# Second layer of a graph network: scores and context as half-array tiles of TensorE, one per graph

## What is computed

```python
q = heads(x @ Wq + bq); k = heads(x @ Wk + bk); v = heads(x @ Wv + bv)   # 6 heads of 128
scores = einsum('bhqd,bhkd->bhqk', q, k) / sqrt(128)     # per graph: 64 x 64
probs  = softmax(scores + where(adj, 0.0, -9e15), axis=-1)
ctx    = einsum('bhqk,bhkd->bhqd', probs, v)
x      = layernorm(x + ctx.reshape(...) @ Wf + bf)
```

## Time and profile before

| | |
|---|---|
| median of three runs | 3291.2 us |
| lowest, highest | 3290.34, 3293.18 us |
| profiled execution, span from first to last instruction | 3285.7 us |
| PE busy | 3071.5 us, 93% |
| weight loads (PEld) busy | 2970.4 us, 90% |
| DVE busy | 1692.9 us, 52% |
| ACT busy | 1407.6 us, 43% |
| mean granted TensorE clock | 0.985 |

### The profile page before, as it was taken

The page is one execution under the profiler, slowest core; times in us unless marked ns, Lnnn a source line. Parts: engine busy times, 40 slices in busy tenths (PEclk is TensorE's granted clock), DMA queues, the critical chain, the costliest instruction groups (busy, mean ns, idle before and its releaser), DMA issues.

```text
span 3285.7 us, 55951 instructions
## 1 busy us (share of the span) xinstructions
PE 3071.5 (93%) x20800; PEld 2970.4 (90%) x20800; DVE 1692.9 (52%) x3820; ACT 1407.6 (43%) x4261; POOL 843.8 (26%) x457
## 2 busy tenths in 40 slices
PE   6999999999999994699999999999999999999998
PEld 6888888888888883699999999999999999999998
DVE  4777777777777775342343433433423334334334
ACT  4677666766676665322322323223223223232232
POOL 2555655565556554000000000000000000000000
PEclk9999999999999996799999999999999999999999
DMA  2111111111111112201010010010010100100100
GB/s 97 40 39 39 44 43 39 39 44 43 39 39 44 44 39 71 94 24 36 21 40 20 21 40 20 21 40 20 25 35 20 40 21 20 40 21 21 39 20 20
DMA packets 60261, 120.07 MB, mean 37 GB/s; under 512 B 22208, under 2 KB 22208, under 8 KB 60096
## 3 DMA queue, kind: packets, MB, share of 16 engines
q1 hardware_dynamic: 60096, 117.50, 10.5%
HBM read 67.15 MB, written 50.33 MB: 36 GB/s over the span
## 4 chain that ended last, share of the span: by engine, by line
PE 54%; DVE 2%; ACT 2%; DMA 1%; issue 1%; SPq 0%; DVEq 0%; ACTq 0%
PE L_ps_k L117 13%; PE L_ps_q L117 13%; PE L_ps_a L117 12%; PE L_ps_a L954 10%; PE L_ps_s L917 3%; PE L_ps_c L937 2%; ACT L_probs L723 1%; DVE L_cT_lo L812 1%; ACT L_cT_hi L709 1%; DVE L_logits L788 1%; PE L_ps_q L871 0%; PE L_ps_s L871 0%; PE L_ps_k L871 0%; PE L_ps_pt L924 0%; DVE L_neg_max L794 0%
## 5 line engine op out<-in xcount | busy, mean ns | idle before, releaser
L681 POOL TENSOR_TENSOR L_x_tok<-L_x_tok,L_bf_all 128x768 f32<-128x768 f32 x64 | 116.5, 1840 | 1793.3 <-PE L_ps_s L871 1793.3
L788 DVE SCALAR_TENSOR_TENSOR L_logits<-L_ps_s,L_mask 64x256 f32<-64x256 f32 x192 | 81.0, 422 | 804.3 <-PE L_ps_s L917 801.3
L117 PE MATMUL L_ps_k<-L_xT_hi,L_w_hi 128*128 128x256 f32 x1152 | 331.1, 287 | 0.0
L117 PE MATMUL L_ps_q<-L_xT_hi,L_w_hi 128*128 128x256 f32 x1152 | 328.5, 285 | 0.0
L117 PE MATMUL L_ps_k<-L_xT_hi,L_w_lo 128*128 128x256 f32 x1152 | 326.0, 283 | 0.0
L117 PE MATMUL L_ps_q<-L_xT_hi,L_w_lo 128*128 128x256 f32 x1152 | 326.0, 283 | 0.0
L117 PE MATMUL L_ps_k<-L_xT_lo,L_w_hi 128*128 128x256 f32 x1152 | 325.9, 283 | 0.0
L117 PE MATMUL L_ps_q<-L_xT_lo,L_w_hi 128*128 128x256 f32 x1152 | 325.9, 283 | 0.0
L745 ACT COPY L_v_tok<-L_ps_a 128x384 f32<-128x384 f32 x128 | 61.3, 479 | 556.8 <-PE L_ps_a L117 556.8
L323 ACT ACTIVATE L_probs<-L_logits,L_neg_max 128x64 f32<-128x64 f32 x768 | 256.2, 336 | 94.5 <-DVE L_neg_max L446 94.5
L117 PE MATMUL L_ps_h<-L_w_hi,L_xT_hi 128*128 128x384 f32 x768 | 271.2, 353 | 21.2 <-DVE L_w_lo L106 21.2
(11 more groups left out here) (119 smaller groups left out, 8156.3 us busy)
## 6 DMA issues: line engine op xcount, KB each, us to landing
L_x_tok<-x SPq DMA_DIRECT2D x64, 384.0 KB, 2.8
x_scratch<-L_x_out SPq DMA_DIRECT2D x64, 384.0 KB, 2.3
L_x_tok<-x_scratch SPq DMA_DIRECT2D x32, 768.0 KB, 4.2
out<-L_x_tok SPq DMA_DIRECT2D x32, 768.0 KB, 3.4
L_stage<-W SPq DMA_DIRECT2D x6, 384.0 KB, 5.2
L_stage<-H_t SPq DMA_DIRECT2D x6, 384.0 KB, 4.0
L_x_tok<-Wq SPq DMA_DIRECT2D x6, 384.0 KB, 3.6
L_x_tok<-Wk SPq DMA_DIRECT2D x6, 384.0 KB, 3.7
```

The lines of the kernel that those rows point to most:

```text
L117: ins = pe.matmul(out, left[a][c], right[b][c], start=(n == 0), stop=(n == len(terms) - 1))
L681: pool.tensor_tensor(x_tok[:, s, t], x_tok[:, s, t], bf_all[:, :], ALU.add).then_inc(biased, 1)
L788: dve.scalar_tensor_tensor(out=logits[r].rearrange("p (h t) m -> p h t m", t=GT), in0=ps_s[r, :].rearrange("p (h t m) -> p h t m", h=2, t= ...
```

## The change

Scores are computed per graph: for each head and tile two matmuls, one for each graph, with 64 columns of the stationary operand and 64 moving ones. The first graph's output lies in partitions 0 to 63, the second's in 64 to 127, so they are two tiles of 128 rows by 64 columns of the array. All scores of a pair now fill 128 partitions by 256 columns; `ps_s` and `ps_pt` are the halves of one bank, `ps_sp`. Context is likewise two matmuls, with a contraction over the graph's 64 nodes (64 rows by 128 columns of the array), all 128 head columns as the stationary side and 64 moving ones; the two graphs write to two banks of `ps_c`. `probsT` is 64 wide, without zeros, and its memset goes. Logits are one instruction. `context_hi` reads both banks in one instruction per head, `context_lo` has one instruction per head and tile. Scores wait for the copies of the preceding pair's transposed probabilities, since they share its bank.

```diff
-        ps_q, ps_k, ps_s, ps_pt, ps_c = (psum(n) for n in ("ps_q", "ps_k", "ps_s", "ps_pt", "ps_c"))
+        ps_q, ps_k, ps_sp = (psum(n) for n in ("ps_q", "ps_k", "ps_sp"))
+        ps_s, ps_pt = ps_sp[:, 0:2 * P], ps_sp[:, 2 * P:4 * P]
+        ps_c = ctx.enter_context(nc.psum_tensor("L1_ps_c", [P, 2, 512], F32))
...
-                for g in range(2):
-                    r = slice(g * NODES, (g + 1) * NODES)
-
-                    dve.scalar_tensor_tensor(
-                        out=logits[r].rearrange("p (h t) m -> p h t m", t=GT),
-                        in0=ps_s[r, :].rearrange("p (h t m) -> p h t m", h=2, t=GT)[:, :, :, r],
-                        scalar=SCALE1, in1=mask[r, s].unsqueeze(1).to_broadcast([NODES, 2, GT, NODES]),
-                        op0=ALU.mult, op1=ALU.add).then_inc(logit_done, 1)
-                dve.wait_ge(logit_done, 2 * (PAIRS * G + j + 1))
+                dve.scalar_tensor_tensor(
+                    out=logits.rearrange("p (h t) m -> p h t m", t=GT),
+                    in0=ps_s.rearrange("p (h t m) -> p h t m", h=2, t=GT),
+                    scalar=SCALE1, in1=mask[:, s].unsqueeze(1).to_broadcast([P, 2, GT, NODES]),
+                    op0=ALU.mult, op1=ALU.add).then_inc(logit_done, 1)
+                dve.wait_ge(logit_done, PAIRS * G + j + 1)
...
-                    dve.scalar_tensor_tensor(out=cT_lo[:, a, :], in0=ps_c[:, h * GN:(h + 1) * GN],
-                                             scalar=bv_col[:, a:a + 1], in1=cT_hi[:, a, :].bitcast(F32),
-                                             op0=ALU.add, op1=ALU.subtract).then_inc(c_lo, 1)
+                    for t in range(GT):
+                        dve.scalar_tensor_tensor(out=by_graph(cT_lo[:, a, :])[:, t], in0=context_of(h)[:, t],
+                                                 scalar=bv_col[:, a:a + 1],
+                                                 in1=by_graph(cT_hi[:, a, :].bitcast(F32))[:, t],
+                                                 op0=ALU.add, op1=ALU.subtract).then_inc(c_lo, 1)
...
+                if j > 0:
+                    pe.wait_ge(ptc_act, 2 * (PAIRS * G + j))
+                    pe.wait_ge(ptc_dve, 2 * (PAIRS * G + j))
                 for h in range(2):
                     for t in range(GT):
-                        n = slice(t * P, (t + 1) * P)
-                        ins = pe.matmul(ps_s[:, (h * GT + t) * P:(h * GT + t + 1) * P], qT[:, j % 2, h, n],
-                                        kT[:, h, n], start=True, stop=True)
+                        for g in range(2):
+                            n = slice(t * P + g * NODES, t * P + (g + 1) * NODES)
+                            k = h * GT + t
+                            ins = pe.matmul(ps_s[g * NODES:(g + 1) * NODES, k * NODES:(k + 1) * NODES],
+                                            qT[:, j % 2, h, n], kT[:, h, n], start=True, stop=True)
...
-                        a = 2 * j + h
-                        ins = pe.matmul(ps_c[:, h * GN + t * P:h * GN + (t + 1) * P],
-                                        v_tok[:, t, a * E1:(a + 1) * E1], probsT[:, h * GT + t, :],
-                                        start=True, stop=True)
+                        for g in range(2):
+                            a, k = 2 * j + h, h * GT + t
+                            m = slice(g * NODES, (g + 1) * NODES)
+                            ins = pe.matmul(ps_c[:, g, k * NODES:(k + 1) * NODES],
+                                            v_tok[m, t, a * E1:(a + 1) * E1], probsT[m, k, :],
+                                            start=True, stop=True)
```

More of the change, by code:

```diff
@@ L592, in layer1 @@
         row_inv = sb("row_inv", [P, PN])
-        probsT = sb("probsT", [P, PN, P])
+        probsT = sb("probsT", [P, PN, NODES])
         cT_hi = sb("cT_hi", [P, KC, GN], F32R)
@@ L612, in layer1 @@
         o_bank = [1, 2, 0, 1]
-        ps_x = [ps_q, ps_k, ps_s]
+        ps_x = [ps_q, ps_k, ps_sp]
         x_in = [sem(f"x_in{s}") for s in range(2)]
         stored = [sem(f"stored{s}") for s in range(2)]
-        consts_in, memsets, ident_ok, bd_zero = (sem(n) for n in ("consts_in", "memsets", "ident_ok", "bd_zero"))
+        consts_in, memsets, ident_ok = (sem(n) for n in ("consts_in", "memsets", "ident_ok"))
         xT_done, hi_done, lo_done = sem("xT_done"), sem("xT_hi_done"), sem("xT_lo_done")
@@ L688, in copy_block, with context_of, by_graph @@
             s = slice(g * NODES, (g + 1) * NODES)
-            out_ = probsT[s, :, s].rearrange("p (h t) n -> p h t n", t=GT)[:, :, t, :]
-            src_ = ps_pt[t * NODES:(t + 1) * NODES, 0:2 * P].rearrange("p (h n) -> p h n", h=2)[:, :, s]
+            out_ = probsT[s, :, :].rearrange("p (h t) n -> p h t n", t=GT)[:, :, t, :]
+            src_ = ps_pt[t * NODES:(t + 1) * NODES, :].rearrange("p (h n) -> p h n", h=2)[:, :, s]
             copy(out_, src_).then_inc(signal, 1)
+        def context_of(h):
+            return ps_c[:, :, h * P:(h + 1) * P].rearrange("p g (t n) -> p t g n", t=GT)
+        def by_graph(sb_head):
+            return sb_head.rearrange("p (t g n) -> p t g n", t=GT, g=2)
         @block.scalar
@@ L695, in _ @@
             w_split_hi(act)
-            act.wait_ge(bd_zero, 1)
             act.wait_ge(consts_in, 64)
@@ L732, in context_hi @@
                 act.wait_ge(c_done, PAIRS * G + j + 1)
-                heads_out([cT_hi[:, 2 * j + h, :] for h in range(2)], ps_c, bv_col, j, c_hi)
+                for h in range(2):
+                    a = 2 * j + h
+                    act.activation(by_graph(cT_hi[:, a, :]), context_of(h), ACT.Identity,
+                                   bias=bv_col[:, a:a + 1]).then_inc(c_hi, 1)
             transposed_hi(0)
@@ L739, in body @@
                 if not first:
-                    act.wait_ge(logit_done, 2 * PAIRS * G)
+                    act.wait_ge(logit_done, PAIRS * G)
                 act.activation(mask[:, s], adj_u8[:, s], ACT.Copy, scale=-MASKED1, bias=MASKED1).then_inc(mask_done, 1)
@@ L768, in _ @@
         def _(dve):
-            dve.memset(probsT[:, :, :], 0.0).then_inc(bd_zero, 1)
             w_split_lo(dve)
-            dve.wait_ge(bd_zero, 1)
             dve.wait_ge(consts_in, 64)
@@ L932, in context @@
                 if j > 0 or not first:
-                    pe.wait_ge(c_lo, 2 * (PAIRS * G + j))
+                    pe.wait_ge(c_lo, PN * (PAIRS * G + j))
                 for h in range(2):
                     for t in range(GT):
-                        a = 2 * j + h
-                        ins = pe.matmul(ps_c[:, h * GN + t * P:h * GN + (t + 1) * P],
-                                        v_tok[:, t, a * E1:(a + 1) * E1], probsT[:, h * GT + t, :],
-                                        start=True, stop=True)
+                        for g in range(2):
[4 more added lines that the diff above has]
+                                            start=True, stop=True)
                 ins.then_inc(c_done, 1)
@@ L948, in output @@
                         pe.wait_ge(o_added, 2 * GT * G + 1)
-                pe.wait_ge(c_lo, 2 * (PAIRS * G + pair + 1))
+                pe.wait_ge(c_lo, PN * (PAIRS * G + pair + 1))
                 left = nodes(cT, n // 2)
```

## The result

The changed kernel takes 3295.47 us (median of 20 runs, 3293.57 to 3297.0), the kernel before, in runs beside it, 3291.07 us (20 runs). The ratio is 1.0015, its 95% interval [1.0008, 1.0022]: by the bound of 0.2% no change, with a loss of about 4 us. The forecast was 3320 us, slower; the time lies in the range of 3260 to 3390.

What follows compares the result with a forecast made beforehand. TensorE's queue was taken to bound the kernel. Per group, 0.70 us for seven switches plus 0.19 for the third pair gave 0.89, times 32 groups 28.5 us: 3320 us forecast, slower, range 3260 to 3390.

Steps and rivals of the forecast that it cites:

- What bounds the kernel: Whole kernel: TensorE's own queue sets the time, busy 93% of the span; the third pair's window is bound by a chain.
- I take 0.055 us for both: Tiled scores and context: each load-and-matmul pair costs 0.055 us, half the old pitch, so neither set changes: term 0.
- the lower end: Tiled scores: two tiles wholly side by side with half the columns each, 0.028 us a pair, a set of 0.45 us.
- Rival B: Tiled context: weight loads go one behind the other, 0.111 us each, +0.89 us at contexts 0 and 2; 3377 us, chance 0.25.
- Rival C: Tiled scores and context: issue of a pair is the limit, +5.34 us a group, 3462 us; chance 0.06.
- A switch at 0.10 us: PE entering or leaving a tiled mode: 0.10 us each, range 0 to 0.26, seven paid a group, +0.70 us.
- the restart row: PE after the wait at 2480.54: second product follows after 0.27 us where 0.17 is usual, +0.10 us.
- The window: Third pair of heads, scores 2 to the load after `context_lo`: 5.68 us, bound by a chain, changing by +0.19 us.
- Logits -0.45: Third pair, DVE: one logits instruction over 128 partitions in place of two saves 0.45 us a group.
- `context_lo` +0.30: Third pair, DVE: four instructions of 128 columns, not two of 256, take 1.18 us against 0.88, +0.30 us.
- The wait +0.34: Before scores 2: waiting for ACT's copies of the preceding pair makes them come 0.34 us later.
- Rival A: Tiled scores: column tiles load and compute side by side, -0.46 us a group, 3276 us, if switches cost under 0.17; chance 0.27.

## Why the prediction was wrong

- **What bounds the kernel**: right. Every stretch that moved lies on PE's path, or in the third pair's window, which stayed bound by its chain through DVE and ACT.
- **"I take 0.055 us for both"** is the step that failed, for the scores. Measured are 0.031 us: the lower end was 0.028, and it was the right one. I halved once, for the smaller load or for the overlap, where both hold: a tile of 64 columns alone costs 0.058 us and two that alternate 0.031. That is 0.40 us a set and 1.2 us a group, more than the whole forecast of 0.89. For the context the same number was right (0.056), and so was its reason, two loads of 128 columns side by side: one tile alone costs 0.112 us. Rival B, loads one behind the other, fell with it. The rule of the Trainium skill (TensorE: Matmul & The Clock Gate, Part 3) that a load overlaps a running matmul of another row group agrees with the 0.056 against 0.112 us of two tiles and one. The scores' tiles share their rows, and they overlapped too, 0.031 against 0.058. Rival C, the issue of a pair as limit at 0.111, fell too.
- **A switch at 0.10 us** was mis-sized: 0.15 us, from 0.30 for a pair of them in the change and 0.31 in the run with more switches. The true price lay in the range of 0 to 0.26. That a switch is not free agrees with the drain that the Trainium skill names (TensorEngine Tiling (Array Packing), Key Properties). I had priced it by the restart row, in which the array was empty already; that the difference of 0.05 us is the emptying is argued, not shown.
- **The window** of the third pair: the sum +0.19 has three terms. Logits -0.45: right (0.45). `context_lo` +0.30: 0.25. The wait +0.34: right in size (0.34) for the tiled scores; in the untiled kernel it measured 0.52, because PE's load comes 0.22 us after the late semaphore and not 0.03, so two errors nearly cancelled, the lag of 0.22 and the 0.18 that the switch covers. That the switch lies under the wait was right. The scores' own gain, left at zero with the first step, is -0.27 (scores in tiles with two logits instructions, 5.76 against 6.03 us). The window measured -0.14.
- With the measured prices the same sum gives 2 x -0.40 for the scores of pairs 0 and 1, 7 x 0.15 for the switches and -0.14 for the window: +0.11 us a group, +3.5 us, and 4.4 were measured. Rival A had the right mechanism and said that its gain lasts only while a switch costs under 0.17 us. At 0.15 its own sum gives -0.11 us a group; it measured about +0.11, because a set fell by 0.40 and not 0.45 (two sets, +0.10) and the window gained 0.14 and not 0.26. I had given it 0.27. That 3295 us lies inside the stated range is in part luck: the missing gain of the scores (-1.07 with the window's share) and the dearer switches (+0.35) were errors in opposite directions.

## What to carry to other kernels

Half-array tiles paid here only where the change also shrank the loaded side (64 weight columns: a set from 0.90 to 0.50 us) and not where it kept 128 columns and halved the rows (0.90 to 0.90); every change of mode between them and full-array products cost 0.15 to 0.17 us, so a short tiled set among full products has to gain 0.3 us before it gains anything. Order the instructions so that neighbours are of different tiles. And take a change apart: its parts here were worth -28 us (scores), +12 (the shared bank) and +22 (context), the first alone was the better kernel, and what was gained on the chain behind the scores (one DVE instruction in place of two) was as large as what the array gained.

## What was not expected of the hardware

A wait that is not the last in PE's list costs more than its own time: with the late semaphore third of four waits PE loaded 0.22 us after it (in tiled and untiled mode), with it last 0.11 us, and where PE has a single wait, behind `context_lo`, 0.05 us. 4 us of the kernel hung on that order.

Two half-array tiles start their rows 0.007 us apart, and they did so even where three rows of the first tile still stood ahead of the second tile's first on the queue. A tile of 64 rows and 128 columns, used alone, has the full array's pitch of 0.112 us.
